# Router, experts and projections as plain fp32 products, and another order of the stacking transfers

## What is computed

```python
def _L0_ffn_ref(tokens, router_w, router_b, expert_weights):       # E = 8, TOP_K = 2
    logits = jnp.einsum('bsh,eh->bse', tokens, router_w) + router_b
    probs = jax.nn.softmax(logits, axis=-1)
    top_p, top_i = jax.lax.top_k(probs, TOP_K)
    w = top_p / (jnp.sum(top_p, axis=-1, keepdims=True) + EPS)
    ...
    y_all = jnp.einsum('nh,ehd->ned', x, expert_weights)           # every token, every expert
    y_k = jnp.take_along_axis(y_all, idx[:, :, None], axis=1)
    out = jnp.einsum('nk,nkh->nh', wf, y_k)
    ...
def _L0_attn_ref(x, wq, wk_down, wv_down, wk_up, wv_up, wo):       # 8 heads, 2 kv heads, latent 32
    q = (x @ wq).reshape(Bq, Tq, N_KV, N_REP, HEAD_DIM)
    k = einsum(x @ wk_down, wk_up); v = einsum(x @ wv_down, wv_up) # in short
    scores = jnp.einsum('bqhrd,bkhd->bhrqk', q, k) * scale         # causal, softmax over k
    ...
x = x + 0.5 * ffn(layernorm(x)); x = x + attn(layernorm(x)); x = x + 0.5 * ffn(layernorm(x))
```

## Time and profile before

| what | us |
|---|---|
| median of 3 runs | 727.15 |
| the 3 runs | 719.2, 729.8, 727.15 |
| the profiled execution's own time | 725.95 |
| its span in the trace | 724.1 |
| PE busy in the span | 559.3 |
| DVE busy | 426.6 |
| ACT busy | 357.5 |
| GpSimd busy | 154.5 |

### The profile page before, as it was taken

How to read it: one execution, slowest core, us unless ns; L and a number is a source line. 1 busy time by engine, 2 the same in 40 slices (tenths; PEclk the granted TensorE clock), 3 DMA queues, 4 the chain that set the end, 5 groups by cost and what they waited for, 6 DMA issues and landing times. The chain is left out here.

```text
span 724.1 us, 10881 instructions
## 1 busy us (share of the span) xinstructions
PE 559.3 (77%) x3526; PEld 277.5 (38%) x3526; DVE 426.6 (59%) x1538; ACT 357.5 (49%) x843; POOL 154.5 (21%) x257
## 2 busy tenths in 40 slices
PE   2726578998987689888994779989894888897935
PEld 2625243344432334344342343434432433343323
DVE  5462765786655475775563456866753577565225
ACT  3233262466665445756463534657653546467612
POOL 2131200143001002510013201531012220043313
PEclk9957667699999689998697697999998899999957
DMA  4002010000110000011000000001100000000000
GB/s 122 0 14 56 15 40 17 1 17 16 45 45 6 18 1 1 16 34 48 24 1 23 16 15 1 1 5 42 44 1 23 16 16 1 1 17 14 16 0 16
DMA packets 23818, 14.59 MB, mean 20 GB/s; under 512 B 5640, under 2 KB 23632, under 8 KB 23760
## 3 DMA queue, kind: packets, MB, share of 16 engines
q1 hardware_dynamic: 23184, 13.49, 6.9%
q10 hardware_dynamic: 576, 0.39, 0.2%
HBM read 3.78 MB, written 2.10 MB: 8 GB/s over the span
## 5 line engine op out<-in xcount | busy, mean ns | idle before, releaser
L706 ACT ACTIVATE prob<-bank,exp_scale 128x512 f32<-128x512 f32 (+3 forms) x384 | 214.9, 583 | 248.7 <-PE bank L1186 183.7
L926 DVE CUSTOM_DVE_ANT_0 masked<-bank,mask_qk 128x128 f32<-128x128 f32 (+3 forms) x256 | 122.7, 486 | 110.6 <-PE bank L1170 109.6
L1170 PE MATMUL bank<-k_stack,q_stack 96*128 96x512 f16 (+3 forms) x384 | 138.6, 366 | 41.5 <-DVE m_part L929 11.9
L1183 PE MATMUL bank<-q_stack,k_stack 98*128 98x512 f16 (+3 forms) x384 | 136.0, 361 | 35.9 <-DMA q_stack<-mT_lo 30.4
L929 DVE TENSOR_REDUCE m_part<-bank 128x1 f32<-128x512 f32 x128 | 87.5, 684 | 72.1 <-PE bank L1170 71.7
L575 POOL TENSOR_TENSOR pair_sum<-dve_sum,scaled 128x256 f32<-128x256 f32 x64 | 46.9, 733 | 282.9 <-DVE dve_sum L899 265.0
L1202 PE MATMUL bank<-prob,v_lat 128*32 128x512 f32 (+3 forms) x768 | 90.6, 546 | 0.5 <-ACT prob L706 0.5
L1205 PE MATMUL bank<-prob,ones 128*32 128x512 f32 (+3 forms) x768 | 87.0, 528 | 0.0
L1183 PEld LDWEIGHTS bank<-q_stack,k_stack 98*128 98x128 f16 x384 | 38.5, 101 | 120.8 <-issue 48.5
L664 ACT ACTIVATE scaled<-bank,gate 128x128 f32<-128x128 f32 x256 | 72.7, 373 | 20.7 <-PE bank L1097 6.6
L1095 PE MATMUL bank<-we_hi,xT_hi 128*128 128x512 f32 x128 | 67.9, 531 | 16.6 <-ACT scaled L664 12.1
(11 more groups left out here) (132 smaller groups left out, 705.6 us busy)
## 6 DMA issues: line engine op xcount, KB each, us to landing
q_stack<-q_hi SPq DMA_DIRECT2D x120, 32.0 KB, 1.8
x<-in_L_attn_x SPq DMA_DIRECT2D x8, 256.0 KB, 2.9
out_x<-x SPq DMA_DIRECT2D x8, 256.0 KB, 2.4
q_stack<-q_lo SPq DMA_DIRECT2D x60, 32.0 KB, 1.9
k_stack<-k_hi SPq DMA_DIRECT2D x32, 32.0 KB, 1.8
prob<-in_L_ffn_expert_weights SPq DMA_DIRECT2D x1, 512.0 KB, 4.3
x<-in_L_attn_wq SPq DMA_DIRECT2D x1, 512.0 KB, 6.0
x<-in_L_attn_wo SPq DMA_DIRECT2D x1, 512.0 KB, 7.0
```

Source lines behind the costliest of these rows:

```text
L706: nc.scalar.activation(into, bank[ST + n % NST][:, 0:w], ACT.Exp, scale=exp_scale[:, 0:1]).then_inc(p_ready, 1)
L926: V.tensor_tensor_reduce(out=masked[:, m % 2, 0:w], in0=seen, in1=mask_qk[:, CH - w:CH], op0=ALU.add, op1=ALU.max, scale=1.0, scalar=LOWES ...
L1170: mm(into[:, 0:w], q_stack[0:MROW, c, g * NR + r, (i % TC) * P:(i % TC + 1) * P], k_stack[0:MROW, b % 2, g, k:k + w], start=True, stop=Tru ...
L1183: last = mm(into[:, 0:CH - off], k_stack[:, b % 2, g, j * P:(j + 1) * P], q_stack[:, c, g * NR + r, off:CH], start=True, stop=not on_diago ...
```

## The change

Two edits. First, each product of parts becomes one plain fp32 product: `three` becomes one `mm` on fp32 operands; the low parts, their DVE subtractions and their semaphores go; ACT's copy of the transposed chunk stays, now to fp32; the weights are loaded straight into their fp32 buffers. The router writes 8 columns for a tile in place of 16, `routing` has one step less, and pieces of `QUICK` behind the copy move one slot ahead. Second, `stack_slot` plans the queries of a quad no earlier than two slots after the last score of that quad in the batch before. That leaves the first two quads where they were, spreads those of the third over slots 66, 69, 72 and 75, and moves those of the last from slots 69 to 72 to slots 98, 101, 104 and 107. In batch 0 nothing moves.

```diff
-GATE_STEPS = 27
+GATE_STEPS = 26
...
+def stack_slot(n, g, r, planned):
+
+    b, c = divmod(n, NC)
+    q = c * NKV + g
+    free = (b - 1) * NS + QSTART[q] + NR * QTILES[q] + 2 + 3 * r
+    return max(planned, free) if b else planned
...
             for _r in range(NR):
-                PLAN["stack_queries", _k + 1 + _r].append((_n, _g, _r))
+                PLAN["stack_queries", stack_slot(_n, _g, _r, _k + 1 + _r)].append((_n, _g, _r))
...
-        xT_hi = sb("xT_hi", [P, 4, CH], F32R)
-        xT_lo = sb("xT_lo", [P, 4, CH], F32R)
+        xT = sb("xT", [P, 4, CH])
...
-                copy(xT_hi[:, xt_home(l, n), :], fb_bank(("xt", l, n))[:]).then_inc(xhi_ready[l], 1)
+                copy(xT[:, xt_home(l, n), :], fb_bank(("xt", l, n))[:]).then_inc(xT_ready[l], 1)
...
-            def low_part(l, n):
-                home = xt_home(l, n)
-                dve.wait_ge(xhi_ready[l], n + 1)
-                low(xT_lo[:, home, :], fb_bank(("xt", l, n))[:], xT_hi[:, home, :]).then_inc(xlo_ready[l], 1)
...
-                step(0, None, V.tensor_tensor, s_l, logits[:, :, 0:NE], bias_b, ALU.add)
-                step(1, 0, V.tensor_tensor, p_l, logits[:, :, NE:2 * NE], s_l, ALU.add)
+                step(0, None, V.tensor_tensor, p_l, logits, bias_b, ALU.add)
...
-            def three(dst, lhs, rhs):
-                mm(dst, lhs[0], rhs[0], start=True, stop=False)
-                mm(dst, lhs[0], rhs[1], start=False, stop=False)
-                return mm(dst, lhs[1], rhs[0], start=False, stop=True)
...
-                    into = logits[:, k * 2 * NE:(k + 1) * 2 * NE]
-                    mm(into, hi, rw_parts[:], start=k == 0, stop=False, skip_group_check=True)
-                    last = mm(into[:, 0:NE], lo, rw_parts[:, 0:NE], start=False, stop=k == u.count * TC - 1,
-                              skip_group_check=True)
+                    last = mm(logits[:, k * NE:(k + 1) * NE], x_part(2 * f, n, t * P, (t + 1) * P), rwT[:],
+                              start=True, stop=True)
...
-                three(take_fb(("y", f, n, j))[:], x_part(2 * f, n, t * P, (t + 1) * P),
-                      both(we_hi, we_lo, slice(None), cols(half))).then_inc(y_done, 1)
+                mm(take_fb(("y", f, n, j))[:], x_part(2 * f, n, t * P, (t + 1) * P), we[:, cols(half)],
+                   start=True, stop=True).then_inc(y_done, 1)
...
-                three(into[0:nk, :], (down_hi[:, 0:nk], down_lo[:, 0:nk]), x_part(1, n)).then_inc(k_done, 1)
+                mm(into[0:nk, :], down[:, 0:nk], x_part(1, n), start=True, stop=True).then_inc(k_done, 1)
```

More of the change, by code:

```diff
@@ L61 @@
                           "bn_1 stats_1 power_1 xn_1 xt_1 key query query_step value")
-QUICK = Pace(bn=0, stats=1, stat_slots=2, power=3, xn=4, xt=7, xt_step=0, logits=10, route=11, route_slots=4, y=16,
-             bn_1=4, stats_1=14, power_1=16, xn_1=17, xt_1=20, key=23, query=24, query_step=1, value=27)
+QUICK = Pace(bn=0, stats=1, stat_slots=2, power=3, xn=4, xt=7, xt_step=0, logits=9, route=10, route_slots=4, y=15,
+             bn_1=4, stats_1=14, power_1=16, xn_1=17, xt_1=20, key=22, query=23, query_step=1, value=26)
 WIDE = Pace(bn=0, stats=3, stat_slots=2, power=6, xn=9, xt=14, xt_step=2, logits=20, route=23, route_slots=6, y=33,
@@ L447, in route_bank @@
             nt = u.count * TC
-            part = [home[:, (2 + i) * NT * NE:(2 + i) * NT * NE + nt * NE].rearrange("p (t e) -> p t e", t=nt)
-                    for i in range(4)]
-            small = [home[:, 6 * NT * NE + i * NT:6 * NT * NE + i * NT + nt] for i in range(2)]
-            return home[:, 0:nt * 2 * NE].rearrange("p (t e) -> p t e", t=nt), part, small
+            logits, *part = [home[:, i * NT * NE:i * NT * NE + nt * NE].rearrange("p (t e) -> p t e", t=nt)
+                             for i in range(5)]
+            small = [home[:, 5 * NT * NE + i * NT:5 * NT * NE + i * NT + nt] for i in range(2)]
+            return logits, part, small
         def mx_bank(use):
@@ L727, in _ @@
                 for l, n, half in PLAN["xn_1", s] + PLAN["xn", s]:
[L728 to L729 removed]
                     standardise(l, n, half)
[L731 to L732 removed]
+                for l, n in PLAN["xt_copy_1", s] + PLAN["xt_copy", s]:
+                    keep_transposed(l, n)
                 for n in PLAN["key_parts", s]:
@@ L844, in step @@
                         if i == 0:
+                            if f == 0 and u.n == 0:
+                                dve.wait_ge(rb_loaded, N_DMA)
+                                dve.wait_ge(set_up, NE + 3)
                             dve.wait_ge(logits_done[f], u.n + u.count)
@@ new lines, in routing @@
+                step(11, 10, V.tensor_tensor, p_k, p_k, rank_b, ALU.mult)
+                step(12, 11, V.reduce_max, r1, p_k, AX.X)
+                step(13, 12, V.tensor_tensor, p_2, p_k, per_expert(r1), ALU.is_equal)
+                step(14, 13, V.tensor_tensor, p_l, p_2, s_1, ALU.add)
+                step(15, 14, V.tensor_tensor, s_l, p_l, s_e, ALU.mult)
+                step(16, 15, V.reduce_sum, p_5, s_l, AX.X)
+                step(17, 16, V.scalar_tensor_tensor, out=r4, in0=r4, scalar=EPS, in1=p_5,
+                     op0=ALU.mult, op1=ALU.add)
@@ new lines, in routing @@
+                step(18, 17, V.reciprocal, r4, r4)
+                step(19, 18, V.tensor_tensor, p_5, p_5, r4, ALU.mult)
+                step(20, 19, V.tensor_scalar, r6, p_5, EPS, 2.0, ALU.max, ALU.mult)
+                step(21, 19, V.tensor_scalar, p_7, p_5, EPS, 1.0, ALU.mult, ALU.add)
+                step(22, 20, V.reciprocal, r6, r6)
+                step(23, 21, V.tensor_tensor, p_7, p_7, r4, ALU.mult)
+                step(24, 23, V.tensor_tensor, p_7, p_7, r6, ALU.mult)
+                if lo <= 25 < hi and u.index >= 2:
@@ L1150, in value_projection @@
                 for t in range(TC):
-                    last = three(into[:, t * nk:(t + 1) * nk], x_part(1, n, t * P, (t + 1) * P),
-                                 (down_hi[:, nk:], down_lo[:, nk:]))
+                    last = mm(into[:, t * nk:(t + 1) * nk], x_part(1, n, t * P, (t + 1) * P), down[:, nk:],
+                              start=True, stop=True)
                 last.then_inc(v_done, 1)
```

134 lines of the change are left out of this document (40 added, 94 removed).

## The result

The changed kernel takes **677.15 us** (median of 4 runs, 676.6 to 677.8) against 726.9 us before (4 runs, 719.2 to 729.8): a ratio of 0.933, with a 95% interval of 0.926 to 0.940. The profiled executions span 676.0 and 724.1 us. It is faster, as forecast, but by 50 us and not by 22, and the time lies under the range of 688 to 722 us.

The account below looks back on a forecast made before the run. The prediction took PE as the main limit, DVE next, plus three 9.9 us boundary waits. Terms -28.5 - 5 + 22.4 - 7 - 3 - 0.6 = -21.7 us took the median from 727.15 to 705 us, range 688 to 722.

Parts of the forecast that it names:

- part 2: Three fp32r products become one plain fp32 product: 28.0 us more PE work, +22.4 us on the path, bounds 14 and 43.
- Part 1: SP's queue at three batch boundaries: maxima ahead of the last quad's queries, 28.5 us of waiting gained, plus 5 behind it.
- the wait only moves: Rival at the batch boundaries: early maxima find something else late, the 28.5 us return, 734 us; chance 0.06.
- the 5 put on the clock there: Low-clock stretches after the three boundary waits, 14.15 us in all: 5 us gained, bounds 0 and 7.1.
- the share of 0.8: Part of the plain products' 28.0 us of added PE work taken to lie on the path, giving +22.4 us.
- Part 3: 24 DVE subtractions of low parts, 0.685 us each, go: -7 us, bounds -4 and -12, plus a clock effect of -3.
- second effect: Clock fall after PE's 2.03 us idle at 338 us may not come without low parts: -3 us, bounds 0 and -8.
- part 4: Small things: weight parts at the start gain 0; one `routing` step less in the three `QUICK` units, -0.6 us.
- The clock helps: Rival: low-clock stretches go almost entirely, PE's added work hides half behind ACT and DVE, 684 to 690 us; chance 0.1.
- The products eat the gain: Rival: PE so full that all 28 us of added product work show at the upper price, 43 us, giving 732 us; chance 0.2.
- slower: the clock: Rival: longer products find the clock low most of the time, +26 us, 753 us; chance 0.04.

Follow-up runs that it names:

- e1_order: The kernel before with only the new order of query rows on SP's queue, all products and low parts kept; 695.9 us, ratio 0.951.
- e6_bank_after: `e1_order` with a transposed chunk planned to hold its PSUM bank one slot instead of two, low parts issued one slot earlier; 684.4 us.
- e7_low_bank: `e4_low_kept` with the new plan of banks of `e6_bank_after`; plain products, low parts still made and waited for, old pace; 689.0 us.
- e9_again: Second run of the kernel after with the pace of the four single-chunk units put back one slot later; 676.6 us.
- after_again: The kernel after, unchanged, run once more beside `e9_again`; 676.5 us.
- e12_after_filler: The kernel after plus an overwritten plain fp32 product of 128 columns ahead of each of the 128 expert products; 700.7 us.
- e11_two_fillers: `e1_order` plus two overwritten products of 128 columns ahead of each of the 128 expert triples; 712.6 us.
- e5_bank_before: The kernel after with a transposed chunk again planned to hold its PSUM bank two slots instead of one; 688.7 us.
- e4_low_kept: `e1_order` with plain fp32 products, while every low part is still made and waited for; 701.4 us.
- e8_filler: `e1_order` plus one overwritten product of 128 columns ahead of each of the 128 expert triples; 697.5 us.
- e10_filler_wide: `e1_order` plus one overwritten product of 256 columns ahead of each of the 128 expert triples; 698.6 us.
- e3_no_low: `e1_order` with three products kept but no low part of a chunk made, the high part read instead; 684.9 us.

## Why the prediction was wrong

The step that failed is the "+22.4 us" of part 2: the price of the product and, with it, what the product does to the clock. It measured +5 to +7.5 us. The plan of the banks, which the forecast left out, gave 9 to 11.5 us more. The medians, one kernel against the next, add up to the whole. Each line is one kernel against the one above it:

| step | kernel | median | step measured | step forecast |
|---|---|---|---|---|
| | before | 728.1 | | |
| order of the rows | `e1_order` | 695.9 | -32.1 | -33.5 |
| plan of the banks (and low parts a slot earlier) | `e6_bank_after` | 684.4 | -11.5 | none |
| plain products | `e7_low_bank` | 689.0 | +4.6 | +22.4 |
| low parts, router, one step of routing | `e9_again` | 676.6 | -12.4 | -10.6, with the pace |
| pace | `after_again` | 676.5 | 0 | |
| sum | | | -51.5 | -21.7 |

Of the 29.8 us between the two sums, 17.8 are the products and 11.5 the row of the banks (some 5 of them at the start, from the earlier low parts or chance); the low parts add 1.8 and the order takes 1.4 back. The medians move by 2 or 3 us with the choice of runs, above all those of kernels with triples (`e1_order` ran from 690.5 to 701.8 us), so each step has that much doubt. Without the highest run of `e1_order` and of `e6_bank_after` the first three steps are -34.2, -11.3 and +6.4, and the fourth stays.

**Part 1, the order: right.** The boundaries gave 10.1 us each in `e1_order`, and 10.1, 9.2 and 9.2 in the kernel after, for a forecast of 9.5 each: nothing of the wait came back. The twelve slots behind them gained 0.3, 0.9 and 1.4 us in `e1_order`, 2.7 for the 5 put on the clock there. The maxima DMAs follow DVE at once, the last quad's queries were not late, and the clock behind the boundary is full. The rival "the wait only moves" is out.

**Part 2, the plain products: the wrong term of the sum.** It was mis-sized by 15 to 18 us, in two pieces: the first is measured, the second an estimate.
The first is the price. The forecast took the triple from two that stood in a row, 0.70 us, while nearly all stand behind other work and take 0.82. With the measured prices, and the low shares that the forecast used, an expert product costs 0.89 x 0.095 + 0.11 x 0.42 = 0.13 us more, 17 us for 128; a query or key product 0.69 x 0.08 + 0.31 x 0.4 = 0.18, 4 us for 24. The value projection's saving was sized well: from its start to the next start 0.84 us in most places (the eight records below, in the kernel after) for 1.37, so about the 3.4 of the forecast.

```profile
196.01 1.00 PE L1106 MATMUL bank<-down,xT 128*128 128x64 f32 x8
196.85 0.38 PE L1138 MATMUL bank<-q_stack,k_stack 98*128 98x512 f16 x1
```

Together that is 18 us of PE and not 28, and at 0.8 it is 14 us. "Starts in a row 0.87 us apart" was right (0.859) and the sum still wrong: the price that was off was that of the thing removed.
The second is the clock. With the plain products, the time at the low clock fell from 168 us to 144 (from 162 without that run of 701.8 us). What a microsecond of it costs can be read from the spread of one kernel: the 25 runs of the kernel before in the first three groups of experiments lie between 717.7 us at a clock of 0.884 and 733.8 us at 0.854, which is 166 and 214 us at the low clock. 16.1 us for 47.6 is 0.34 for each, and a line through all 25 gives 0.34 too. (The four to six runs of the other kernels give 0.1 to 0.6, and two runs of the kernel before in the fourth group, 747.0 and 784.6 us at 0.764 and 0.696, 0.1 to 0.2.) So 18 to 24 us less are worth 6 to 8 us, and the 6 to 8 us that are left of 14 stand beside the 5 to 7.5 measured. That is an estimate: no run holds the clock still. By the same reckoning the share of 0.8 isn't settled. At an equal low clock the work costs (5.5 + 8) / 18 = 0.75 here and (24 - 2) / 28 = 0.78 in `e12_after_filler`, but only 0.5 to 0.6 in the three kernels with filler in `e1_order`, as (15.9 + 2) / 29.2 in `e11_two_fillers`.
That added work on PE can lower the time at the low clock was seen with filler too, of another kind (-17 us). Why, the runs don't settle: the sum of PE's idle between the first and last score was 70.5 us in `e1_order` and 70.3 us with filler, so it isn't that idle vanished.

**Part 3, the low parts: the size right, the second effect laid to the wrong cause.** 11 and 12.4 us were measured for 10.6 forecast (with part 4). But "with 0.69 us less to wait such a fall may not come" is refuted: without any low part the idle of 2.03 us stayed. It came from a bank's holder. How much of the 8.8 us at slots 156 to 168 the banks gave depends on the clock that followed: 0.8 us between `e1_order` and `e6_bank_after`, 3.8 between `e5_bank_before` and the kernel after, 7.0 between `e4_low_kept` and `e7_low_bank` (23.4 to 16.4, the latter at 0.95). At slots 192 to 204 the three pairs give 4.5, 4.3 and 3.0 us.

**The step that was left out.** The forecast went through the instructions that the change adds and removes. The two lines in the planner add and remove none, and in them lay 9 to 11.5 us, more than in any term of the sum but the two largest. The evidence stood in the trace: the transposes at 339.97 us wait for `q_lo`, which doesn't read a transposed chunk. A wait for a reader of another value is a wait for a buffer.

**The rivals.** "The clock helps" (684 to 690 us, chance 0.1) is nearest, in its mechanism as well: the low clock fell from 190 to 111 us, which at 0.34 us each, the estimate above, is 27 of the 50 us. That counts across the terms (the waits, the banks and the products each take part of it), and it isn't a term beside them. It didn't go almost entirely, as the rival had it. "The products eat the gain" and "slower: the clock" rested on the price of the product and fell with it.

## What to carry to other kernels

Price a removed operation where it stands: between other work, not from the densest row in the trace. When a diff touches a planner (how long a buffer is held, a slot, a due time), run the old and the new plan and compare who follows whom in each buffer; an idle whose releaser doesn't produce what the waiting instruction reads shows where that matters. And add up what two or three terms make of the clock as one term, from the spread of the runs of one kernel, before giving each edit a full-clock price.

## What was not expected of the hardware

**The low clock costs less than half of its time.** 0.34 us for each microsecond at 1.2 GHz, by the runs of one kernel. The Trainium skill ("TensorE: Matmul & The Clock Gate", Part 1, section "HAM oscillation — how this bites in real kernels") reckons the penalty as low time x (1 - 1.2/2.4), so 0.5. The measurement is lower. A reason that fits, though no run tries it alone: in the profiled execution of the kernel before, PE was busy for only 132 of its 190 us at the low clock, and 0.5 x 132 / 190 is 0.35.

**What a product costs depends on its neighbours.** Means from start to next start, in us, of the groups between other work at the full clock:

| kernel | filler | first of the triple | second, third | whole |
|---|---|---|---|---|
| `e1_order` | | 0.353 | 0.233, 0.234 | 0.82 |
| `e8_filler` (128 columns) | 0.180 | 0.285 | 0.234, 0.234 | 0.93 |
| `e10_filler_wide` (256 columns) | 0.240 | 0.234 | 0.233, 0.235 | 0.94 |

All three products of the triple have 512 columns, and the first costs 0.35 us behind other work, 0.29 behind a filler of 128 columns and 0.23 behind one of 256. The wider filler took 0.06 us longer itself, and the product behind it gave nearly all of that back. So twice the columns cost 0.01 us in the whole. In `e10_filler_wide`, and then in `e11_two_fillers` with its two fillers ahead:

```profile
510.95 0.36 PE L1140 MATMUL bank<-we_hi,xT_hi 128*128 128x256 f32 x1
511.15 0.39 PE L1104 MATMUL bank<-we_hi,xT_hi 128*128 128x512 f32 x1
511.38 0.40 PE L1105 MATMUL bank<-we_lo,xT_hi 128*128 128x512 f32 x1
```

```profile
520.40 0.31 PE L1141 MATMUL bank<-we_hi,xT_hi 128*128 128x128 f32 x1
520.55 0.28 PE L1142 MATMUL bank<-we_hi,xT_lo 128*128 128x128 f32 x1
520.66 0.45 PE L1104 MATMUL bank<-we_hi,xT_hi 128*128 128x512 f32 x1
520.95 0.40 PE L1105 MATMUL bank<-we_lo,xT_hi 128*128 128x512 f32 x1
```

The starts are 0.20 and 0.23 us apart in the first, and 0.15, 0.11 and 0.29 in the second. The load of a 128x128 fp32 stationary is recorded with 0.21 us in the kernel before. That it shows where the product ahead is shorter than itself fits all these rows, and wasn't tried by itself.

**The spread is the clock's.** `e1_order`, `e3_no_low` and `e6_bank_after`, with triples, spread over 11 to 15 us, and within each the shorter runs have the higher clock (681.1 us at 0.896 and 695.9 at 0.871 for `e3_no_low`). Kernels with plain products mostly spread less (1.1 us for the kernel after at first, 8.3 us when it ran again), but so did `e8_filler`, with triples (1.6 us).

**A level between the two.** The 0.95 in the profiled execution of `e7_low_bank` (above) is neither of the clock's two levels, held for 556 us. None of the other fifteen profiled executions has it. What set it off stays open.
